# A four-layer graph network on one core: the edge features' copy moved from ScalarE's queue to SyncE's, and epsilon moved into the square root

## The reference, cut to what matters

```python
h = max(layernorm(x, eps=1e-5), 0);  x = x + sage(sage(h))          # mean over the edges, two convolutions
h = max(layernorm(x, eps=1e-5), 0);  x = x + segment_sum((h @ W)[src] * edge_weight, dst) + b
h = max(layernorm(x, eps=1e-5), 0);  x = x + interaction(h, edge_attr_64)   # eps=1e-6 in its two norms
h = max(layernorm(x, eps=1e-5), 0);  x = x + h @ W_self + mean over the edges of top32(h @ W_neigh)
```

## Time and profile before

| what | value |
|---|---|
| median of the runs | 1990.85 us (1989.31 to 1990.9) |
| the profiled execution's own time | 1990.57 us |
| its span, first to last instruction | 1988.8 us |
| PE busy | 1721.3 us (87%) |
| DVE busy | 1142.3 us (57%) |
| ACT busy | 738.0 us (37%) |
| POOL busy | 366.8 us (18%) |
| mean granted TensorE clock | 0.947 |

### The profile page before, as it was taken

How to read it: one execution, slowest core, us unless ns; L and a number is a source line. 1 busy time by engine, 2 the same in 40 slices (tenths; PEclk the granted TensorE clock), 3 DMA queues, 4 the chain that set the end, 5 groups by cost and what they waited for, 6 DMA issues and landing times.

```text
span 1988.8 us, 47501 instructions
## 1 busy us (share of the span) xinstructions
PE 1721.3 (87%) x11659; PEld 1284.9 (65%) x11660; DVE 1142.3 (57%) x3359; ACT 738.0 (37%) x2169; POOL 366.8 (18%) x980
## 2 busy tenths in 40 slices
PE   2599998999991999999997999999888888884996
PEld 1255554555550777768886888888666655662886
DVE  5488887888888122223335666666367776775111
ACT  0588988999882111111111222222122222221000
POOL 1255554555553000000000000000011111110000
PEclk7799999999996999999998999999899999996998
DMA  9442432332335565543334665565221111110444
GB/s 242 139 141 100 140 109 100 114 135 100 121 128 146 146 179 170 165 149 113 118 132 121 169 182 156 162 182 165 70 69 51 51 64 56 51 51 17 146 150 147
DMA packets 302014, 246.01 MB, mean 124 GB/s; under 512 B 143658, under 2 KB 285798, under 8 KB 301926
## 3 DMA queue, kind: packets, MB, share of 16 engines
q1 hardware_dynamic: 251686, 231.82, 37.7%
q10 hardware_dynamic: 50240, 13.37, 2.9%
HBM read 138.17 MB, written 99.31 MB: 119 GB/s over the span
## 4 chain that ended last, share of the span: by engine, by line
issue 61%; PE 23%; ACTq 4%; DVE 4%; ACT 2%; POOL 2%; DVEq 2%; SPq 0%; POOLq 0%; DMA 0%
PE ps L1242 15%; PE ps L1292 7%; ACTq L578 3%; POOL work L562 2%; ACT front L592 2%; DVE front L830 1%; DVE front L828 1%; ACT work L586 1%; ACTq L328 0%; DVE work L951 0%; PE ps L1227 0%; DVE arena L962 0%; PE ps L1273 0%; ACTq L337 0%; DVE arena L822 0%
## 5 line engine op out<-in xcount | busy, mean ns | idle before, releaser
L1292 PE MATMUL ps<-arena 128*128 128x256 f16 (+1 forms) x5000 | 598.9, 274 | 48.3 <-POOL arena L552 38.8
L1292 PEld LDWEIGHTS ps<-arena 128*128 128x128 f16 x5000 | 488.0, 98 | 146.7 <-issue 78.2
L1242 PE MATMUL ps<-front 128*128 128x400 bf16 x2580 | 482.0, 340 | 49.1 <-ACT front L592 46.0
L592 ACT ACTIVATE front<-front 128x128 bf16<-128x128 bf16 x1290 | 407.3, 390 | 56.4 <-issue 32.6
L1242 PEld LDWEIGHTS ps<-front 128*128 128x128 bf16 x2580 | 240.2, 99 | 222.1 <-ACT front L592 57.6
L540 POOL TENSOR_SCALAR front<-front,w_col 128x128 bf16<-128x128 bf16 x645 | 245.7, 387 | 190.2 <-DVE front L828 184.6
L1286 PE MATMUL ps<-arena 128*128 128x256 f32 x1250 | 280.4, 381 | 0.0
L562 POOL TENSOR_TENSOR work<-work 128x256 f32<-128x256 f32 x75 | 55.7, 743 | 1104.6 <-ACT work L695 1104.6
L1286 PEld LDWEIGHTS ps<-arena 128*128 128x128 f32 x1250 | 237.0, 191 | 31.6
L830 DVE TENSOR_SCALAR front<-iota,off_g,front 128x400 bf16<-128x400 f16 x645 | 253.9, 394 | 0.0
L828 DVE TENSOR_SCALAR front<-iota,front 128x128 bf16<-128x128 f16 x645 | 162.9, 253 | 115.6 <-PE ps L1242 94.6
(11 more groups left out here) (179 smaller groups left out, 1461.4 us busy)
## 6 DMA issues: line engine op xcount, KB each, us to landing
arena<-turned_blocks SPq DMA_DIRECT2D x75, 800.0 KB, 4.3
wgt_blocks<-arena SPq DMA_DIRECT2D x25, 1600.0 KB, 8.5
arena<-wgt_blocks SPq DMA_DIRECT2D x25, 1600.0 KB, 8.2
cnt_blocks<-work SPq DMA_DIRECT2D x25, 800.0 KB, 4.2
turned_blocks<-arena SPq DMA_DIRECT2D x25, 800.0 KB, 3.5
e_raw<-edge_features_padded SPq DMA_DIRECT2D x25, 576.0 KB, 7.8
edge_features_padded<-in_edge_attr ACTq DMA_DIRECT2D x1, 12480.0 KB, 61.0
out<-arena SPq DMA_DIRECT2D x24, 128.0 KB
```

Of the source, the lines that this page charges most:

```text
L592: m = act.activation(part_of(u, O_SW + a * P, P), part_of(u, O_S, P), ACT.Copy, scale=one(col[:, c, :], t))
L1242: return pe.matmul(out_, left, right, start=False, stop=True, skip_group_check=True)
L1292: m = pe.matmul(agg[par][:, 0:wide], BLK16[par][:, b * P:(b + 1) * P], ZH[zin(i)][:, b * ZW + part * D:b * ZW + part * D + wide], start=(b ...
```

## The change

SP issues the copy of the edge features instead of ACT: `pad_edges(c)` stands at the head of `store(c, par)`, so SP issues a piece of 16 edge tiles (512 KB) before it waits for chunk c's blocks, 24 times, and for the last chunk the rest (6 edge tiles, the partial one and the two padding fills). ACT's four DMAs and its wait for the indices are gone. The square root reads the variance and takes epsilon as its bias, from two columns that POOL sets at the start; DVE's tensor_scalar is gone, and with it two drains in `outer_and_top`; `bn_aggr` itself raises `s_var`. The last norm waits for the free row before the square root instead of after the reciprocal, and the reciprocal follows line 1157 without a drain. DVE, PE and now ACT wait for nine constants instead of seven.

```diff
+EPIECE = (ET - 1) // (NT - 1)
@@ sync
+            def pad_edges(c):
+                if not isinstance(c, int):
+                    sp.dma_start(eap_dram[:, bass.ds(c * EPIECE, EPIECE), :],
+                                 edge_attr[bass.ds(c * (EPIECE * P), EPIECE * P), :].rearrange("(t p) f -> p t f", p=P)
+                                 ).then_inc(s_eapad, 16)
+                    return
+                at = c * EPIECE
+                sp.dma_start(eap_dram[:, at:ET - 1, :], edge_attr[at * P:(ET - 1) * P, :].rearrange(
+                    "(t p) f -> p t f", p=P)).then_inc(s_eapad, 16)
+                sp.dma_start(eap_dram[0:ER, ET - 1, :], edge_attr[(ET - 1) * P:E, :]).then_inc(s_eapad, 16)
+                sp.wait_ge(s_pad, 4)
+                sp.dma_start(eap_dram[ER:P, ET - 1, :], e_raw[ER:P, 0, :]).then_inc(s_eapad, 16)
+                sp.dma_start(eap_dram[:, ET:EPAD, :], e_raw[:, 0:EPAD - ET, :]).then_inc(s_eapad, 16)
+
             def store(c, par):
+                pad_edges(c)
                 wait(sp, s_taken, c * PER + (PER + CR))
...
-            sp.wait_ge(s_eapad, 16 * 4)
+            sp.wait_ge(s_eapad, 16 * (NT + 3))
@@ gpsimd
+            pool.memset(eps_outer, LN_EPS).then_inc(s_const, 1)
+            pool.memset(eps_inner, LN_EPS_INTER).then_inc(s_const, 1)
@@ scalar
-            act.wait_ge(s_rows, 16 * 3 * (EB + 1))
-            act.dma_start(eap_dram[:, 0:ET - 1, :], edge_attr[0:(ET - 1) * P, :].rearrange("(t p) f -> p t f", p=P)
-                          ).then_inc(s_eapad, 16)
-            act.dma_start(eap_dram[0:ER, ET - 1, :], edge_attr[(ET - 1) * P:E, :]).then_inc(s_eapad, 16)
-            act.wait_ge(s_pad, 4)
-            act.dma_start(eap_dram[ER:P, ET - 1, :], e_raw[ER:P, 0, :]).then_inc(s_eapad, 16)
-            act.dma_start(eap_dram[:, ET:EPAD, :], e_raw[:, 0:EPAD - ET, :]).then_inc(s_eapad, 16)
...
-            def deviation(k):
+            def deviation(k, eps=eps_outer):
                 wait(act, s_var, k + 1)
-                act.activation(sd, ve, ACT.Sqrt).then_inc(s_std, 1)
+                act.activation(sd, mv[:, 1:2], ACT.Sqrt, bias=eps).then_inc(s_std, 1)
@@ vector
-            def variance(eps):
-                return dve.tensor_scalar(ve, mv[:, 1:2], eps, None, ALU.add).then_inc(s_var, 1)
-
-            def inverse_deviation(k):
-                wait(dve, s_std, k + 1)
-                return dve.reciprocal(rs, sd)
-
-            def norm(rows_, into, eps, k):
+            def spread():
+                dve.bn_aggr(mv, bn).then_inc(s_var, 1)
+
+            def scaled(rows_, into, k):
+                wait(dve, s_std, k + 1)
+                chain(dve.reciprocal(rs, sd))
+                return dve.tensor_scalar(into, rows_, mv[:, 0:1], rs, ALU.subtract, ALU.mult)
+
+            def norm(rows_, into, k):
                 chain(dve.bn_stats(bn, rows_))
-                chain(dve.bn_aggr(mv, bn))
-                variance(eps)
-                chain(inverse_deviation(k))
-                return dve.tensor_scalar(into, rows_, mv[:, 0:1], rs, ALU.subtract, ALU.mult)
+                spread()
+                dve.drain()
+                return scaled(rows_, into, k)
...
                 dve.drain()
                 if outer:
-                    dve.bn_aggr(mv, bn)
+                    spread()
                 if top:
                     dve.tensor_copy(span(ZH[0], (n - 2) * ZW, D), top_row)
                 dve.drain()
-                if outer:
-                    variance(LN_EPS)
                 if top:
                     dve.tensor_tensor(span(ZH[0], (n - 2) * ZW + D, D), top_row, span(ZH[0], (n - 2) * ZW, D),
                                       ALU.subtract).then_inc(s_zD, 1)
-                dve.drain()
                 if outer:
-                    inverse_deviation(k + 1)
-                    dve.drain()
                     hrow_free(g - 1)
-                    dve.tensor_scalar(hrow[1 - par], last, mv[:, 0:1], rs, ALU.subtract, ALU.mult).then_inc(s_row, 1)
+                    scaled(last, hrow[1 - par], k + 1).then_inc(s_row, 1)
```

More of the change, by code:

```diff
@@ L139, in build @@
         mv_all = work[:, 1, 0:2 * NT].rearrange("p (n s) -> p n s", s=2)
-        ve_all, sd_all, rs_all = (work[:, k, 0:NT] for k in (2, 3, 4))
+        sd_all, rs_all = (work[:, k, 0:NT] for k in (3, 4))
         mean_own = work[:, 6:8, :].rearrange("p a d -> p (a d)")
@@ L143, in build @@
         small = sb("small", [P, 32], F32)
-        bn, mv, ve, sd, rs, mx8 = (small[:, 0:6], small[:, 6:8], small[:, 8:9], small[:, 9:10], small[:, 10:11],
-                                   small[:, 16:24])
+        bn, mv, sd, rs, eps_outer, eps_inner, mx8 = (small[:, 0:6], small[:, 6:8], small[:, 9:10], small[:, 10:11],
+                                                     small[:, 11:12], small[:, 12:13], small[:, 16:24])
         scale_f = sb("scale", [P, 3, 12], F32)
@@ L638, in row_phase @@
                 z(NT - 1, g0 + NT - 1, (g0 + NT - 1) % 2)
+            act.wait_ge(s_const, 9)
             act.wait_ge(s_var, 1)
-            act.activation(sd_all, ve_all, ACT.Sqrt).then_inc(s_std, 1)
+            act.activation(sd_all, mv_all[:, :, 1], ACT.Sqrt, bias=eps_outer).then_inc(s_std, 1)
             with act.Fori(0, NT // SB) as j:
@@ L712, in inter @@
                 if back1:
-                    deviation(n * 3 + (ln0 - 5) if not (isinstance(n, int) and n == 1) else ln0)
+                    deviation(n * 3 + (ln0 - 5) if not (isinstance(n, int) and n == 1) else ln0, eps_inner)
                 if here:
@@ L718, in inter @@
                 if back2:
-                    deviation(n * 3 + (ln0 - 4) if back1 else ln0 + 3 * NT - 2)
+                    deviation(n * 3 + (ln0 - 4) if back1 else ln0 + 3 * NT - 2, eps_inner)
                 if back1:
@@ L741, in _ @@
             dve.wait_ge(s_pad, 3)
-            dve.wait_ge(s_const, 7)
+            dve.wait_ge(s_const, 9)
             whole = "p c e -> p (c e)"
@@ L953, in _ @@
             for n in range(NT):
-                dve.bn_aggr(mv_all[:, n, :], bn_all[:, n, :])
+                m = dve.bn_aggr(mv_all[:, n, :], bn_all[:, n, :])
+            m.then_inc(s_var, 1)
             dve.drain()
-            dve.tensor_scalar(ve_all, mv_all[:, :, 1], LN_EPS, None, ALU.add).then_inc(s_var, 1)
             dve.wait_ge(s_std, 1)
@@ L1005, in pre_sage2 @@
                 chain(dve.tensor_tensor(node(X, n), node(X, n), urow, ALU.add))
-                norm(node(X, n), hrow[par], LN_EPS, n + 1).then_inc(s_row, 1)
+                norm(node(X, n), hrow[par], n + 1).then_inc(s_row, 1)
             def post_sage2(n, g, par):
@@ L1032, in pre_gcn @@
                 chain(dve.tensor_tensor(node(X, n), node(X, n), urow, ALU.add))
-                chain(norm(node(X, n), urow, LN_EPS, n + NT + 1))
+                chain(norm(node(X, n), urow, n + NT + 1))
                 dve.tensor_scalar(node(R_, n), urow, 0.0, None, ALU.max)
@@ L1081, in inner @@
                 wait(dve, s_tv, n)
-                chain(norm(urow, inner_row, LN_EPS_INTER, ln0 if isinstance(n, int) and n == 0 else n * 3 + (ln0 - 2)
+                chain(norm(urow, inner_row, ln0 if isinstance(n, int) and n == 0 else n * 3 + (ln0 - 2)
                            ).then_inc(s_inner, 1))
@@ L1114, in outer_and_top @@
                 dve.drain()
-                if outer:
-                    variance(LN_EPS_INTER)
                 if top:
@@ L1196, in _ @@
             pe.sem_inc(s_agg, CR)
-            pe.wait_ge(s_const, 7)
+            pe.wait_ge(s_const, 9)
             pe.wait_ge(s_prep, PREP_ROWS)
```

5 lines of the change are left out of this document (1 added, 4 removed).

## The result

The median of the changed kernel is 1967.69 us (1965.63 to 1969.1, four runs) beside 1990.88 us for the kernel before on the same chip: a ratio of 0.9882, 95% interval 0.9865 to 0.9899. It is faster, as forecast, but 8.4 us above the forecast of 1959.3 and 1.7 us above the range. The profiled execution took 1968.69 us, 21.88 us less than that of before; the forecast had 31.3.

What follows compares the result with a forecast made beforehand. It took the copy on ACT's queue to cost 26 us at the start. From 1990.57 us it subtracted 26.0 (copy), 1.2 (serial ends), 3.4 (long tiles) and 0.7 (outer norm), 31.3 together, giving 1959.3; range 1946 to 1966.

Steps and rivals of the forecast that it cites:

- the build, put at nothing: Build phase: SP's added pieces were costed at 0, with a few us kept for the range.
- the serial ends: Norm over all tiles, stage ends, first inner norm, last interaction tile: five gains of 0.15 to 0.3 us, 1.2 us together.
- The copy leaves ACT: Start: without the copy on its queue ACT's first one-hot moves from 72.68 to 46.6 us, a gain of 26.0 us.
- Pieces at SP cost nothing: Build: 24 pieces of 512 KB, 2.4 us each, are covered by SP's wait for ACT; cost 0.
- The rival of the held SP: Build: pieces over 8.5 us delay SP's stores; at 10 us each the time is 1995 us; chance 0.03.
- a disturbed build: Build rival: a fifth of each piece's time shows, 12 us, time 1971; chance 0.10; sign, a build over 530 us.
- ACT's square root with a bias is the same instruction: Every norm: taking epsilon as bias was to leave ACT's square root unchanged.
- Long tiles, 0.31 us each: Interaction, last norm: L1164 starts at 1499.40 instead of 1499.71, 0.31 us in 11 long tiles, 3.4 us.
- a shorter wait of PE gives fewer slow tiles: Interaction, in the race's rival: PE's wait and the cause of four slow L1273 tiles shrink, 6.3 us.
- Short tiles, 0.7 us by the outer norm: Interaction: L1124 comes 0.07 us earlier, POOL's sum stretches 0.06 us less, 11 times, 0.7 us.
- The race: Interaction long tiles: L1124 leads POOL's sum by 0.12 us instead of 0.05, which hardly suffices for DVE to win.
- its rival: Interaction long tiles: DVE wins the port, long tiles become short, 12.3 us more, time 1947; chance 0.33.

Runs made afterwards that it cites:

- the copy alone: Kernel before with only the edge-feature copy moved to SP in pieces, epsilon staying on DVE: 1966.83 us, ratio 0.9877.
- the one-piece copy: Changed kernel with SP issuing the whole copy at once behind the loads of x, ahead of the first store: 1991.77 us, ratio 1.0003.
- the filled build: PE's wait filled, plus sixteen products of zeros at the start of each of the build's 25 chunks: 1953.32 us, ratio 0.9809.
- the copy and the order: The copy alone, with the last norm dropping the drain behind line 1157 and awaiting its free row first: 1964.34 us, ratio 0.9864.
- every piece twice: Changed kernel with each of the 24 pieces issued a second time into a DRAM tensor nobody reads: 1967.3 us, ratio 0.9883.
- PE's wait filled: The copy and the order, plus ten unread products of zeros per interaction tile before PE waits for DVE's rows: 1954.85 us, ratio 0.9816.
- the outer norm alone: The copy alone, with epsilon moved from DVE into the square root's bias for the outer norm only: 1948.76 us, ratio 0.979.
- the early wait: Changed kernel with ACT's wait for nine constants moved from before the all-tiles square root to the head of its build: 1965.22 us, ratio 0.9865.
- the inner norm put back: Changed kernel with only the interaction's inner norm restored, DVE adding epsilon and the square root without operand: 1966.78 us, ratio 0.9869.
- the zero bias with the fill: PE's wait filled, with the outer norm's square root alone taking a bias column of zeros: 1951.19 us, ratio 0.9797.
- epsilon alone: Changed kernel with the copy left on ACT's queue, so only epsilon moves into the square root: 1994.41 us over 12 runs, ratio 1.0014.
- the zero as bias: Kernel before with every small square root given a bias column of zeros: 1979.82 us, ratio 0.9941.

## Why the prediction was wrong, and where it was right

The direction and the main mechanism, ACT's queue held by the copy, were right. The time was missed by no single step but by three terms of the sum: the build, put at nothing (3.5 us); the interaction phase, whose gain in plain long tiles was eaten by two more tiles with a slow L1273 (3.6); and the serial ends, with a square root called unchanged and a table load overlooked (2.5).

- **The copy leaves ACT: right,** and closer than it deserves: 26.12 us against 26.0. The way from the table to the first one-hot was taken as 3.24 us and is 3.60 (3.60 to 3.62 in all kernels with the copy off ACT), but the table was ready 0.40 us sooner than before. Over those kernels it is ready between 42.96 and 44.70, and the first one-hot follows. The rule that issuing from another engine saves only the time to initiate, which the prediction cites from the Trainium skill, "DMA: Bandwidth & Descriptors", section "Issuing engines are not separate DMA queues", and weighs, does not hold for this copy: the kernel before and the copy alone are 24 us apart (1990.9 and 1966.8).
- **Pieces at SP cost nothing: right,** and doubled they cost nothing still. The rival of the held SP was right in its mechanism: with the copy in one piece it eats the whole gain. Its threshold was wrong. It added up the times to landing and let a piece cost something from 8.5 us on; a piece takes 9.5 us to land, which by that reckoning would have cost about 1 us in each chunk. The 2.4 us that it took for a piece are neither its time to landing nor its hold on SP's queue (0.8 to 1.5 us). What counts is that hold beside SP's wait for ACT.
- **The build, a term that the sum put at nothing, is the first step that failed.** From ACT's first one-hot to its last block it takes 532.6 us, and took 529.2: 3.5 us more. The granted clock, read in stretches of 2 us, stood at the 1.2 GHz level for 41 us of it, in 10 spells (the one in which the build begins included); before it was 32 us in 8. Over the kernels (the one-piece copy and the filled build aside) the length goes with this time at the low level and not with the pieces. With 31 to 32 us the build takes 527.9 to 529.2 (the copy and the order, every piece twice, PE's wait filled, the outer norm alone, and the kernel before, which has no pieces); with 35 to 38 us, 530.3 to 531.6 (the copy alone, the early wait, the inner norm put back, the zero bias with the fill, and epsilon alone, without pieces); with 41 us, 532.6 to 532.9 (the changed kernel, and the zero as bias, without pieces). The number of spells by itself does not order them: 9 go with 528.4 us (PE's wait filled), 8 with 531.3 (the inner norm put back). What sets the clock there stays open. It need not be the change: the four executions of the changed kernel took 1965.63 to 1969.1 us, at mean granted clocks of 0.952 to 0.948, so one and the same kernel varies by this much. My sign for a disturbed build, "longer than 530 us", would have named the wrong cause. The windows from the first one-hot to the last block, changed kernel and then before:

```profile
46.56:579.20 532.64, 489.71 (x3177) 281.58 (x3177) 439.98 (x1483) 472.48 (x1490) 287.88 (x857) 0.96 0.48 142
```

```profile
72.68:601.86 529.18, 486.73 (x3177) 280.97 (x3177) 440.22 (x1484) 471.98 (x1490) 289.28 (x855) 0.97 0.33 112
```

- **"ACT's square root with a bias is the same instruction": wrong.** It takes 0.29 us instead of 0.20, on all 125. The trace of before had a price for an operand, which I did not look for: line 688, with a scale and a bias column, took 453 ns at 128 x 128, line 695, with the bias alone, 363. The Trainium skill, "ScalarE: Activation LUTs", section "What ACT_TABLE_LOAD costs", says that each such column adds about 93 ns; the trace agrees. At a serial end 0.15 us of DVE gives way to 0.09 of ACT; by that the five ends were worth some 0.3 us and not 1.2, an estimate from these two durations.
- **Serial ends: wrong by the table load,** 1.28 us on the path at the first norms. The changed code has a second wait right ahead of the square root; the trace of before shows the load right after ACT's last block. Each was there to be read, though that a second wait would move the load was first shown by the run with the early wait. Of the 2.5 us missed at these ends the load is half, and the other half is the 1.2 us, of which nothing can be seen: from the first product of sage 1 to the first MLP sum the difference grows by 0.03 us.
- **Long tiles, 0.31 us each: right** (0.33), and by the step named, the drain and the free row. **Their sum, 3.4 us: wrong.** Two more of them fell to the slow clock, 2 times 1.69 us. The idea that a shorter wait of PE gives fewer slow tiles holds only in part: the wait went from 1.81 to 1.49 us and the slow tiles from four to six, but there are none where DVE wins the race, which leaves a wait of 0.79, or where the wait is filled.
- **Short tiles, 0.7 us by the outer norm: wrong in sign.** The lead there fell from 0.18 to 0.15 us instead of growing by 0.07, POOL's sum takes 0.84 us instead of 0.81, and the tile 14.60 instead of 14.57. With the outer norm's edit alone the term comes as forecast: a lead of 0.25, a sum of 0.75, a tile of 14.50.
- **The race: the place was right, the lead and the threshold wrong.** I forecast a lead of 0.12 and judged that it hardly suffices, between 0.11 and 0.14. The lead became -0.09, since the sum counted what leaves DVE after the inner norm and neither what ACT's operand adds before it (0.09 to 0.10) nor the step issued 0.11 us later, whose cause is open. And 0.11 suffices: with the outer norm's edit alone the forecast's own condition came about and its rival followed, at 1948.8 us against the 1947 worked out for it; in the interaction phase, 16.7 us against the 16.4 of the forecast's and the rival's terms together.

Together, of the 31.3 us: 0.1 more at the start, 3.5 less in the build, 2.5 less at serial ends (1.2 forecast, 1.3 lost), 3.6 less in the interaction phase (its two terms, 4.1, brought 0.5). That leaves 21.8 us; the two executions are 21.9 apart.

## What to carry to other kernels

A large DMA issued on a compute engine's queue is paid by whatever is issued behind it: put it on a queue with slack, in pieces that fit between its other work. An operand column has a price on ACT (0.09 us here), and a wait added ahead of an activation can pull the load of its table onto the path. Where two engines meet within 0.1 us and one then holds up the other, an edit is worth what the meeting is worth: test its parts one at a time, since the outer norm's part of this change gave 17 to 18 us beside the copy, and nothing in the company of the rest.

## What the runs showed of the hardware

- **The race between DVE's scaled rows and POOL's sum** went to POOL at every lead of up to 0.07 us and at the one of 0.10, and to DVE at 0.11 and above. The loser takes longer: DVE 0.78 to 0.97 us instead of 0.41 (leads of -0.10 to 0.10), POOL up to 0.88 instead of 0.72. The rows show the stretching and not the port itself. The rule of the Trainium skill that the prediction cites ("SBUF — State Buffer", section "SBUF: two separate sides"), that the one that starts first holds the pair, fits these rows only if DVE's claim comes about 0.1 us behind the start that the profile shows.
- **Adding 0.09 us to each small square root made the kernel 11 us faster,** since it moved POOL's sum (0.17 us) more than DVE's rows (0.09).
- **The issue behind a DMA between two DRAM tensors holds its queue:** 58.99 us on ACT and 47.90 on SP behind the copy of 12,480 KB, some 6.4 on SP when a second piece of 512 KB follows the first at once.
- **Short waits of PE are enough for the granted clock to fall.** Waits of 1.49 us in tiles of about 15 us went with a fall in six of eleven; ten products of zeros per tile ended them and gave 9.5 us, and the mean granted clock of the whole profiled execution rose from 0.952 to 0.955.
